# Weight units split by GpSimd instead of ScalarE and VectorE, k's products in a second PSUM bank, a divided last store

## The reference

```python
W = weights[condition]                       # 16 conditions, one number per batch
c = einsum('bct,bcd->bdt', x, W)             # mixes the 64 tokens of a batch
qkv = einsum('bsc,cf->bsf', c, Wqkv) + bqkv  # q, k, v of 256 channels, one head
attn = softmax(einsum('bqd,bkd->bqk', q, k) / 16)
x = x + einsum('bqd,dc->bqc', attn @ v, Wo) + bo
y = einsum('bsi,boi->bso', x, weight[condition])   # a 1024x1024 matrix per condition
out = y @ W.T + b                            # 1024x1024, shared
scores = y @ gate_w.T + gate_b               # 4 ranks: 8, 16, 32, 64; the best one is taken
x = x + out + (y @ A[:r].T @ B[:, :r].T of the best rank)
```

## Time and profile before

| | |
|---|---|
| median of three runs | 2286.02 us (2283.11 to 2287.87) |
| profiled execution, own time | 2283.59 us |
| profiled execution, span | 2281.9 us |
| PE busy | 2246.7 us, 98% |
| PEld, DVE, ACT, POOL busy | 77%, 54%, 42%, 3% |
| DVE in phase A, by 40th of the span | 70 to 79% |
| granted TensorE clock | 0.999 of full speed |
| HBM read and written | 219 and 134 MB |

### The profile page before, as it was taken

How to read it: one execution, slowest core, us unless ns; L and a number is a source line. 1 busy time by engine, 2 the same in 40 slices (tenths; PEclk the granted TensorE clock), 3 DMA queues, 4 the chain that set the end, 5 groups by cost and what they waited for, 6 DMA issues and landing times.

```text
span 2281.9 us, 73807 instructions
## 1 busy us (share of the span) xinstructions
PE 2246.7 (98%) x28506; PEld 1748.9 (77%) x28506; DVE 1236.8 (54%) x3438; ACT 953.2 (42%) x2461; POOL 61.3 (3%) x128
## 2 busy tenths in 40 slices
PE   7999999999999889999999999999999999999998
PEld 4777777777777678887878787878787878787876
DVE  7777777777777754343434444444344444434443
ACT  5776767677767643232322222222222222222221
POOL 4000000000000000000000000000000000000000
PEclk9999999999999999999999999999999999999999
DMA  7668777777677743141214141214225132231303
GB/s 290 249 255 303 272 269 284 272 264 280 245 283 276 271 180 113 44 144 38 93 58 149 39 158 66 76 38 151 74 69 193 39 112 84 103 112 39 131 20 112
DMA packets 108960, 356.46 MB, mean 156 GB/s; under 512 B 27600, under 2 KB 28752, under 8 KB 79184
## 3 DMA queue, kind: packets, MB, share of 16 engines
q1 hardware_dynamic: 98640, 280.89, 34.1%
q0 software_dynamic: 10112, 72.36, 8.5%
HBM read 218.99 MB, written 134.22 MB: 155 GB/s over the span
## 4 chain that ended last, share of the span: by engine, by line
PE 96%; DVE 2%; DMA 1%; ACT 1%; issue 1%; POOL 0%; SPq 0%; DVEq 0%; ACTq 0%; POOLq 0%; PEldq 0%
PE bank L1179 21%; PE bank L1315 19%; PE bank L1284 19%; PE bank L1286 10%; PE bank L1317 10%; PE bank L1136 4%; PE bank L1138 4%; PE bank L1137 4%; PE bank L1297 1%; PE bank L1324 1%; PE bank L1325 1%; PE bank L1299 1%; DMA w<-ws 0%; DVE wf L875 0%; PE bank L1231 0%
## 5 line engine op out<-in xcount | busy, mean ns | idle before, releaser
L1284 PE MATMUL bank<-xs,w 128*128 128x128 f16 x8192 | 625.1, 219 | 3.9 <-DVE xs L882 2.0
L1179 PE MATMUL bank<-w,xs 128*128 128x384 f16 x3072 | 553.2, 327 | 4.4 <-DVE w L895 4.4
L1315 PE MATMUL bank<-y,wf 128*128 128x512 f16 x2048 | 483.8, 379 | 0.8 <-DVE xr L925 0.8
L1284 PEld LDWEIGHTS bank<-xs,w 128*128 128x128 f16 x8192 | 478.2, 98 | 5.8 <-issue 2.4
L763 ACT ACTIVATE zh<-bank 128x256 f32<-128x256 f32 x256 | 97.8, 382 | 777.1 <-PE bank L1286 774.1
L1179 PEld LDWEIGHTS bank<-w,xs 128*128 128x128 f16 x3072 | 290.6, 98 | 165.0 <-issue 2.8
L1286 PE MATMUL bank<-xs,w 128*128 128x64 f16 x8192 | 405.8, 193 | 0.0
L921 DVE SCALAR_TENSOR_TENSOR xr<-bank,xr 128x256 f32 (+1 forms) x256 | 108.6, 424 | 432.7 <-PE bank L1325 387.5
L1315 PEld LDWEIGHTS bank<-y,wf 128*128 128x128 f16 x2048 | 196.9, 98 | 186.6 <-DVE xr L925 1.1
L1286 PEld LDWEIGHTS bank<-xs,w 128*128 128x128 f16 x8192 | 335.9, 98 | 0.0
L1317 PE MATMUL bank<-y,wf 128*128 128x256 f16 x2048 | 265.4, 273 | 0.0
(11 more groups left out here) (158 smaller groups left out, 2083.9 us busy)
## 6 DMA issues: line engine op xcount, KB each, us to landing
stage<-w_in SPq DMA_DIRECT2D x68, 1024.0 KB, 8.8
w<-ws POOLq DMA_DIRECT2D x68, 1024.0 KB, 6.1
ws<-wf SPq DMA_DIRECT2D x64, 1024.0 KB, 6.9
out<-xr SPq DMA_DIRECT2D x128, 256.0 KB, 2.3
xr<-x_in SPq DMA_DIRECT2D x31, 1024.0 KB, 8.0
x<-xr SPq DMA_DIRECT2D x31, 1024.0 KB, 4.4
xr<-x SPq DMA_DIRECT2D x124, 256.0 KB, 3.5
wcf<-wc_in SPq DMA_DIRECT2D x128, 32.0 KB, 4.5
```

Source lines behind the costliest of these rows:

```text
L1179: e = mm(zps[q % 2][h][:, 0:384], lhs, rhs[:, k, h * 384:(h + 1) * 384], start=(k == 0 and lhs is a and rhs is wq_h), stop=(k == K - 1 and ...
L1284: mm(both, hi[:, k, c], x_k, start=(k == 0), stop=False)
L1315: mm(fps[m % 2][:, :], wf_h[:, k, c], yhl[:, u, k, :], start=(k == 0), stop=False)
```

## The change

GpSimd takes over the 68 units. After `write_order` it issues two loads on its own queue and then, for each unit, runs: four `tensor_scalar` of 128x1024 (high part of each half as float16, and the half itself scaled in place in float32), two `tensor_tensor` of 128x1024 (scaled minus high), the store to `ws`, and the load of the unit after next. Loops run over the conditions; the four units of the shared matrix come last. Only then `load_condition(0)` and `first_slots` follow in GpSimd's code, without the `PACE` waits and without the wait on the last z product. ScalarE and VectorE lose all pieces of units, SP loses the loads and stores.

The q half of the qk products stays in bank 4; the k half goes to the bank that the step's own z held (bank 0 or 2). ScalarE signals after two of its four copies, so VectorE can start on q while ScalarE copies k.

Smaller: at the start the second half of the first pair's x is loaded and split behind the eight chunks of Wqkv; TensorE's wait for the chunks of Wo moves from before step 2 into the first output products; the last two chunks are split in steps 2 and 3 instead of phase B; the last group is stored in three pieces of 4, 2 and 2 blocks.

```diff
         zps = [[bank[0], bank[1]], [bank[2], bank[3]]]
-        qkps, chps, wops = bank[4], bank[5], [bank[6], bank[7]]
+        qps, kps, chps, wops = bank[4], [bank[0], bank[2]], bank[5], [bank[6], bank[7]]
...
+        def qk_block(r, c):
+
+            return qps[:, c * P:(c + 1) * P] if c < 2 else kps[r][:, (c - 2) * P:(c - 1) * P]
...
             for n in range(2, 5):
                 load_chunk(n)
-            sp.dma_start(group_cols(0, PT2, PT2), x_in[0, :, PT2:GR]).then_inc(s_x[0], 16)
...
             for n in range(6, K):
                 load_chunk(n)
+            sp.dma_start(group_cols(0, PT2, PT2), x_in[0, :, PT2:GR]).then_inc(s_x[0], 16)
             load_mix(0, 1)
...
-                    unit_turn(*here, load=not late_units)
...
-            store_out(IB - 1, 1)
-            for u in range(2):
-                sp.wait_ge(s_out[u], 64 * IB)
+            rs = batches(IB - 1, 1)
+            for lo, hi in TAIL:
+                sp.wait_ge(s_res, FA + 16 * IB - K + hi)
+                for b, r in enumerate(rs):
+                    sp.dma_start(out[bass.ds(r, 1), :, lo * S:hi * S].rearrange("a p n -> (a p) n"),
+                                 group_cols(GB - 1, b * BT + lo * S, (hi - lo) * S)).then_inc(s_out[1], 16)
...
                 for t in range(TS):
-                    if n == 0:
-                        pool.wait_ge(s_z, PACE * (t + 1))
-                    else:
+                    if n > 0:
                         pool.wait_ge(s_pt[t], 16 * n)
...
-                pool.wait_ge(s_z, NP)
                 pool.wait_ge(s_st[0], 16 * (IA - 1))
...
-            pool.wait_ge(s_wl, K + 4)
-            pool.wait_ge(s_order, 1)
+            def load_unit(i, q):
...
+                pool.dma_start(stage[:, q % 2, :], src).then_inc(s_unit[q % 2], 16)
+
+            def split_unit(i, q, final=False):
+
+                high, low = unit_halves(q, q if final else None)
+                wait(pool, s_unit[q % 2], i, 32, 16 * (q // 2) + 16)
+                pool.sem_inc(s_turn_pool, 1)
...
+                elif not final:
+                    wait(pool, s_us[q % 2], i, 32, 16 * (q // 2))
+                    pool.sem_inc(s_turn_pool, 1)
+                halves = [slice(n, n + T) for n in range(0, UNIT, T)]
+                for c in halves:
+                    st = stage[:, q % 2, c]
+                    pool.tensor_scalar(high[:, c], st, SW, 1.0, ALU.mult, ALU.mult).then_inc(s_uhi, 1)
+                    pool.tensor_scalar(st, st, SW, 1.0, ALU.mult, ALU.mult).then_inc(s_uhi, 1)
+                for h, c in enumerate(halves):
+                    wait(pool, s_uhi, i, 16, 4 * q + 2 * h + 2)
+                    pool.tensor_tensor(low[:, c], stage[:, q % 2, c], high[:, c], ALU.subtract).then_inc(s_ulo, 1)
+
+            def units(i, last=False):
+                for q in range(4):
+                    split_unit(i, q)
+                    wait(pool, s_ulo, i, 8, 2 * q + 2)
+                    dst = ws[bass.ds(i, 1), :, q, :, :].rearrange("a p h n -> (a p) h n")
+                    pool.dma_start(dst, split_w[:, q % 2, :, :]).then_inc(s_us[q % 2], 16)
+                    load_unit(i if q < 2 else i + 1, (q + 2) % 4)
+
+            load_unit(0, 0)
+            load_unit(0, 1)
+            pool.wait_ge(s_sort, S_SEGMENTS + 1)
+            units(0)
+            with pool.Fori(1, NC - 1) as i:
+                units(i)
+            units(NC - 1, last=True)
+            for q in range(4):
+                split_unit(NC, q, final=True)
+                if q < 2:
+                    wait(pool, s_ulo, NC, 8, 2 * q + 2)
+                    load_unit(NC, q + 2)
             load_condition(0)
             first_slots()
...
                 for c in range(4):
-                    e = nc.scalar.activation(qkh[:, c, :], qkps[:, c * P:(c + 1) * P], Iden, bias=biasq[:, c:c + 1])
-                e.then_inc(s_qkh, 1)
+                    e = nc.scalar.activation(qkh[:, c, :], qk_block(q % 2, c), Iden, bias=biasq[:, c:c + 1])
+                    if c % 2 == 1:
+                        e.then_inc(s_qkh, 1)
...
-                unit_hi(i, q, (0,) if end else (2,))
...
-                if not end:
-                    unit_lo(i, q, (2,))
...
                 wait(pe, s_ol, i, 4, 2 * u + 2)
+                if isinstance(i, int) and i == 0 and u == 0 and 0 in ms:
+                    pe.wait_ge(s_wl, K + 4)
+                    pe.wait_ge(s_sort, S_SEGMENTS + 1)
...
             a_step(0, 1)
-            pe.wait_ge(s_wl, K + 4)
-            pe.wait_ge(s_sort, S_SEGMENTS + 1)
             a_step(0, 2)
...
                 if isinstance(i, int) and i == 0 and u == 0 and m == 0:
-                    pe.wait_ge(s_wul, NPC * UNITS)
+                    pe.wait_ge(s_ulo, PART * UNITS)
```

More of the change, by code:

```diff
@@ L422, in body @@
                         store_x1(i - 1, 1)
-                    unit_turn(here[0], here[1] + 1, load=not late_units)
-                    if late_units:
-                        for q in range(2):
-                            load_unit(IA, q)
             body(0, first=True)
@@ L792, in b_step @@
                     gate_exp(pi, pu)
-                if first and q == 0:
-                    for n in range(2):
-                        act.wait_ge(s_us[n], 16 + 16 * UNITS_A // 2)
                 y_set(i, q, 1)
@@ L798, in b_step @@
                     x_hi(i, q + 1, phase_b=True)
-                if first and q == 0:
-                    chunk_hi(K + 4)
-                    chunk_hi(K + 5)
                 y_set(i, q, 2)
                 y_set(i, q, 3)
-                if first and q < 2:
-                    for n in range(2 * q, 2 * q + 2):
-                        unit_hi(IA, n, range(NPC), n)
                 if j == 0 and before:
@@ L867, in _ @@
             assert done[0] == S_SLOT
-            def unit_lo(i, q, pieces, final=None):
-                for c in pieces:
-                    wait(dve, s_wuh, i, 4 * NPC, NPC * q + c + 1)
-                    lo, hi = PIECES[c]
-                    high, low = unit_halves(q, final)
-                    v.scalar_tensor_tensor(out=low[:, lo:hi], in0=stage[:, q % 2, lo:hi], scalar=SW,
-                                           in1=high[:, lo:hi], op0=ALU.mult, op1=ALU.subtract).then_inc(s_wul, 1)
             def x_lo(i, q, b, phase_b=False):
@@ L949, in a_step @@
                     oo(0)
-                else:
-                    unit_lo(i, q, (0, 1))
-                wait(dve, s_qkh, i, 4, q + 1)
+                elif isinstance(i, int) and i == 0 and q >= 2:
+                    chunk_lo(K + 2 + q)
                 for c in range(4):
-                    e = v.scalar_tensor_tensor(out=qkl[:, c, :], in0=qkps[:, c * P:(c + 1) * P],
+                    wait(dve, s_qkh, i, 8, 2 * q + c // 2 + 1)
+                    e = v.scalar_tensor_tensor(out=qkl[:, c, :], in0=qk_block(q % 2, c),
                                                scalar=biasq[:, c:c + 1], in1=qkh[:, c, :], op0=ALU.add,
@@ L957, in a_step @@
                 e.then_inc(s_qkl, 1)
-                if end:
-                    unit_lo(i, q, (0,))
-                else:
+                if not end:
                     mix_lo(i, q + 1)
@@ L1100, in b_step @@
                         x_lo(i, q + 1, b, phase_b=True)
-                if first and q == 0:
-                    chunk_lo(K + 4)
-                    chunk_lo(K + 5)
                 y_set(i, q, 2)
                 y_set(i, q, 3)
-                if first and q < 2:
-                    for n in range(2 * q, 2 * q + 2):
-                        unit_lo(IA, n, range(NPC), n)
                 if before:
```

85 lines of the change are left out of this document (24 added, 61 removed).

## The result

The changed kernel takes **2553.57 us** (four runs, 2549.93 to 2567.86); the kernel before took 2285.11 beside it (four runs). The ratio is 1.1186, interval 1.1141 to 1.1230: 268 us slower, where the prediction had 2360 and 2268 to 2450. The sign was forecast, the size and the path were not, so the sign is luck.

A forecast was written before the change was run, and what follows sets the result against it. The prediction took TensorE to bound the kernel, busy 2246.7 of 2281.9 us. From 2283.6 it added 78 for GpSimd's lateness and subtracted 3 of gains: 2358.6, with the median's 2.4 offset 2361, rounded 2360 us; range 2268 to 2450.

The forecast's parts named there:

- A unit by itself: GpSimd's four scalings, two subtractions, two DMA issues and starts: 10.1 us a unit undisturbed, ends 7.7 and 18.9.
- What VectorE does to it: In phase A, VectorE's instructions with SBUF inputs hold GpSimd still, stretching a unit from 10.1 to 12.0 us.
- the 10.9 that the prediction named as the sign that it is wrong: GpSimd's units in phase A: the forecast is wrong if a unit takes under 10.9 us.
- the 78 us of lateness: First pair of phase B: TensorE's last set starts at 888 us instead of 810, 78 us later.
- The queue behind the last unit: Start of phase B: nine MB of matrices queue behind GpSimd's last unit at 863 us, adding 25.4 us.
- VectorE waits for GpSimd: Phase A steps: VectorE waits until GpSimd's instruction is through, 0.75 us a step, 45 us, so 2320; chance 0.16.
- a mean rest of 0.85 us and up to 2.3: Phase A: what remains of a GpSimd instruction when VectorE meets one, in 8.9 of 12.0 us.
- The gains: Waits at the start, for qkl, around phase B's beginning and at the end: 3 us, or 11 if GpSimd is in time.
- a covered start: TensorE ends phase A earlier but then waits for GpSimd, covering those gains; 3 us remain, from phase B and the end.
- The faster rival: Phase A: units take at most 10.5 us, GpSimd is through by 761 us, total 2275 or 2268; chance 0.27.
- an estimate of 2.25 us for a subtraction: GpSimd's `tensor_tensor` of 1024 columns: half the skill page's 4497 ns for 2048, leaving the unit's sum at 10.0 us.

The follow-up runs named there:

- GpSimd was made late, at 836.4 us: Against the changed kernel: GpSimd waits after each of a unit's six instructions, and SyncE issues mix-matrix loads ahead of its wait for x's store; 2332.91 us.
- a stop and the earlier mix loads: Against the changed kernel: GpSimd scales one column and waits before each six instructions; SyncE's mix-matrix loads precede its wait for x's store; 2315.40 us.

## Why the prediction was wrong

- **A unit by itself: right.** Forecast 10.1 us from the narrow rows, measured 10.09. Scalings 1.05 for 1.07, subtractions 2.1 for 2.3, a store's issue 0.61 for 0.53; the 0.68 us that GpSimd waits for its own last signal stood in the sum with 0.2. That the sum fits so closely is in part luck: it had the instructions too long by about as much as it had this wait too short.
- **What VectorE does to it: the step that failed.** From the earlier trace rows I read that GpSimd stands still while VectorE's two-input instruction runs, and stretched the unit to 12.0 us. The row shows it for a VectorE that is already running. In the changed kernel it was mostly VectorE that stood still: the mean scaling took 1.07 to 1.08 us against 1.05 where VectorE reads nothing of the kind from SBUF, the subtraction 2.16 against 2.12. Where VectorE did get in, a train grew from 8.2 to 9.1 us, but over all units one took 10.3 us, under the 10.9 that the prediction named as the sign that it is wrong. So the 78 us of lateness were not there.
- **The queue behind the last unit: right as a mechanism, not at work.** Where GpSimd was made late, at 836.4 us, the forecast's 25.4 us behind it give 861.8 for the last set of the first pair; it started at 864.69. In the changed kernel GpSimd was through at 743, before even the old end of phase A.
- **The rival "VectorE waits for GpSimd": right mechanism, mis-sized term.** The forecast's own sum had this wait at nothing, "hidden behind GpSimd's lateness"; with the clock behind it, it was the whole loss. As a rival it had a chance of 0.16 and a price of 45 us. Its price rested on "a mean rest of 0.85 us and up to 2.3", the rest of one instruction. What was waited for was the rest of a whole train, 6 to 8.3 us and once 16.1, and the chain met the next train again: the holds of the mix at 425.56 and pn at 435.50 came one behind the other. VectorE's instructions grew by 280 us, TensorE's gaps by 215. Where holds are the rest of one instruction, with a stop and the earlier mix loads, the time was 2315 us, near the rival's 2320, with 27 us of waits for its 45.
- **The clock: missing.** 55 us came from products at the lower clock after the waits. A wait cost about a quarter more than its length.
- **The gains: right in sign and order.** 3 us with a covered start, 11 with none; alone they came to 4.5. **The faster rival** asked for a unit under 10.5 us and VectorE not in the way; with both it got 2279.55 where it said 2275.
- The Trainium skill (GPSIMD Engine Reference, section Performance versus the Vector engine) led to an estimate of 2.25 us for a subtraction; undisturbed it took 2.1 us here. The Trainium skill (SBUF - State Buffer, section Who interferes with whom) says that issue order decides who blocks, and that the first one has the ports for the whole instruction. With a stop ahead of the trains the holds agree with that (at most 2.0 us, against 2.1 of a subtraction). In the changed kernel they don't: 31 holds went on over several instructions to the end of the train, and there the measurement decides.

What is shown: the loss is VectorE's holds (it goes with the instructions that can be held); they last to the end of a train when they start early in one that GpSimd comes to without a stop (31 of 34 in units 1 to 3), and to the end of one instruction when it was stopped by a wait. What isn't: that the loop's jump back is such a stop, why a stop has that effect, and why instructions that start late in a train are let in. No run here looks into either engine's queue.

## What to carry to other kernels

Before work is put on GpSimd beside VectorE, list VectorE's instructions on the critical chain that read only SBUF, and price each with the rest of GpSimd's whole unbroken stretch, not of one instruction; then add the clock that TensorE loses in the waits. If such work has to be there, give VectorE PSUM inputs (all of them, one isn't enough) or stop GpSimd briefly ahead of each stretch. And first ask what the engine that is relieved was holding up: here it was nothing, and the small edits alone had all the gain that these runs can tell.

## What the runs showed of the hardware

- A VectorE instruction of 0.29 us that started 0.27 us before GpSimd's stretch of six took 8.59 us; one that started 0.12 us after a stretch's begin took 8.20. Beside two such stretches without a DMA issue between them one of 0.69 us took 16.78.
- A wait of 0.19 us ahead of the stretch limited the hold to 2.0 us; a like instruction without the wait didn't (8.1 on pn).
- VectorE's instructions with one input in PSUM and the other in SBUF (qkl 0.34 us, xr 0.42), and its reciprocal of one column (0.16 us), kept their lengths beside GpSimd in all runs.
- In the last 8 us of a wait of 14.78 us the granted clock was 0.50; it was 0.52 in the first 4 us of products and 1.00 in the next 4.
